# Relative attention rows stored and loaded with 800 bytes, the constant end filled on chip

## What is computed

```python
q, k, v = proj(Wq, bq), proj(Wk, bk), proj(Wv, bv)          # [B, 16, L, 16]
attn = einsum('bhld,bhrd->bhlr', q, k) * scale
dist = clip(arange(L)[None, :] - arange(L)[:, None], -64, 8) + 64
rel  = einsum('bhld,lrd->bhlr', q, dist_emb[dist]) * scale   # 73 different values a query
attn = softmax(attn + rel, axis=-1)
x = layernorm(x + (attn @ v) @ Wo.T + bo)
```

## Time and profile before

| | |
|---|---|
| median of 3 runs | 1431.49 us (1430.58 to 1434.02) |
| the profiled execution | 1432.69 us, its span 1430.9 us |
| TensorE (PE) busy | 1272.6 us, 89% |
| VectorE (DVE) busy | 1043.6 us, 73% |
| ScalarE (ACT) busy | 947.5 us, 66% |
| GpSimd (POOL) busy | 337.1 us, 24% |
| mean granted TensorE clock | 0.951 |
| moved by DMA | 273.13 MB, mean 191 GB/s |

### The profile page before, as it was taken

How to read it: one execution, slowest core, us unless ns; L and a number is a source line. 1 busy time by engine, 2 the same in 40 slices (tenths; PEclk the granted TensorE clock), 3 DMA queues, 4 the chain that set the end, 5 groups by cost and what they waited for, 6 DMA issues and landing times. The chain is left out here.

```text
span 1430.9 us, 24911 instructions
## 1 busy us (share of the span) xinstructions
PE 1272.6 (89%) x8220; PEld 675.3 (47%) x8220; DVE 1043.6 (73%) x2547; ACT 947.5 (66%) x1666; POOL 337.1 (24%) x567
## 2 busy tenths in 40 slices
PE   7788999999999999999999999999996899910597
PEld 4334344344334334334434434437885687700586
DVE  3366788888887888888888888862574467999655
ACT  4434677777777777777777777773765558959600
POOL 4544121211211211212112121004553002310012
PEclk9988999999999999999999999999998799965799
DMA  8999977878888788698797786625321314825032
GB/s 240 300 339 253 255 222 220 229 206 245 224 221 226 215 244 214 201 265 215 209 251 208 233 223 183 206 75 168 98 71 45 133 59 130 311 87 207 11 108 88
DMA packets 263758, 273.13 MB, mean 191 GB/s; under 512 B 66222, under 2 KB 246990, under 8 KB 259534
## 3 DMA queue, kind: packets, MB, share of 16 engines
q1 hardware_dynamic: 261998, 268.39, 64.7%
q10 hardware_dynamic: 1632, 3.15, 0.7%
HBM read 153.69 MB, written 117.00 MB: 189 GB/s over the span
## 5 line engine op out<-in xcount | busy, mean ns | idle before, releaser
L604 ACT ACTIVATE pr<-scoresT 128x512 f32<-128x512 f32 x1024 | 548.4, 600 | 210.5 <-PE scoresT L856 151.3
L851 PE MATMUL scoresT<-qT,kT 99*128 99x512 bf16 (+7 forms) x1408 | 357.2, 327 | 5.5 <-DVE attn_out L741 2.3
L701 DVE TENSOR_REDUCE mx<-scores_for_max 128x1 f32<-128x888 f32 (+6 forms) x448 | 301.7, 673 | 0.0
L696 DVE CUSTOM_DVE_ANT_0 junk<-scores_for_max,win 128x200 f32<-128x200 f32 (+2 forms) x512 | 180.0, 352 | 158.3 <-PE scores_for_max L823 149.1
L699 DVE TENSOR_REDUCE mx<-scores_for_max 128x1 f32<-128x64 f32 (+6 forms) x448 | 277.5, 619 | 0.0
L869 PE MATMUL attn_out<-pr,vS 128*17 128x512 f32 x2048 | 270.3, 600 | 4.4 <-DMA vS<-v_all 4.2
L851 PEld LDWEIGHTS scoresT<-qT,kT 99*128 99x128 bf16 (+1 forms) x1408 | 107.9, 98 | 334.0 <-ACT rows L581 97.0
L856 PE MATMUL scoresT<-idf,win 128*128 128x128 f32 (+1 forms) x1024 | 201.7, 258 | 0.0
L478 POOL COPY rows<-rows 128x736 f32<-128x736 f32 x128 | 102.5, 800 | 379.3 <-ACT rows L581 379.3
L822 PE MATMUL scores_for_max<-kX,qT 64*128 64x512 bf16 x512 | 167.2, 384 | 3.9 <-DVE mx L701 3.0
L823 PE MATMUL scores_for_max<-kX,qX 64*128 64x512 bf16 x512 | 167.2, 384 | 0.0
(11 more groups left out here) (203 smaller groups left out, 1728.2 us busy)
## 6 DMA issues: line engine op xcount, KB each, us to landing
rel_table<-rows SPq DMA_DIRECT2D x128, 512.0 KB, 4.7
win<-rel_table SPq DMA_DIRECT2D x128, 512.0 KB, 5.4
up_raw<-xT_normed SPq DMA_DIRECT2D x6, 1536.0 KB, 9.2
xT_normed<-up_raw SPq DMA_DIRECT2D x6, 1536.0 KB, 6.6
qT<-q_parts SPq DMA_DIRECT2D x32, 256.0 KB, 7.6
kX<-k_parts SPq DMA_DIRECT2D x64, 128.0 KB, 5.0
kT<-k_parts SPq DMA_DIRECT2D x32, 256.0 KB, 5.6
q_parts<-shared SPq DMA_DIRECT2D x32, 192.0 KB, 4.7
```

Source lines behind the costliest of these rows:

```text
L604: nc.scalar.activation(pr[:, n % NPR, h, :], bank, ACT.Exp).then_inc(t_read, 1)
L696: last = nc.vector.tensor_tensor_reduce(junk[:, n % 2, 0:z - a], bank[:, a:z], win[:, T % NW, q4, h, u:u + z - a], 1.0, NEG, ALU.add, ALU. ...
L701: last = nc.vector.tensor_reduce(mx[:, T % 2, q4, h, 2:3], bank[:, z:L], AX.X, ALU.max)
L851: last = mm(bank[:, a:e], k[0:r], q[0:r, a:e], start=(n == 0), stop=not near and n == len(pieces) - 1, skip_group_check=True)
```

## The change

LP goes from 184 to 128, so a row tile has 200 places a head (NC) in place of 256 and a row of the table 328 in place of 384. A store of a row tile and a load of a window move 800 bytes a row in place of 1024. The loaded 200 values stand at places 56 to 255 of `win` (FLAT = 56). Places 0 to 55 are filled by GpSimd with the value at place 56, for the 72 queries (partitions) that the `before` matmul reads, within shift_of. Those who read the constant at place 0 read it at place 56. `cut_window` and the first score of a tile wait for the fill (w_flat). For the fourth `side` tile, `cut` now also lies 72 queries in, as for the other three: the product is split into 456 and 56 queries, and the transposing matmul has 72 queries.

```diff
--- before.py
+++ after.py
@@ -53,10 +53,11 @@
     LEAD = 8
     CH = 16
     WRAP = RIGHT
-    LP = 184
+    LP = 128
     NC = LP + NJ
     TWID = NC + P
     WID = 2 * P
+    FLAT = P - LEFT - WRAP
     VW = HD + 1
     NEG = -3.0e38
     BLKS = 2 * B
@@ -130,6 +131,7 @@
         o_rec = sem("o_rec")
         r_padded = sem("r_padded")
         w_cut = sem("w_cut")
+        w_flat = sem("w_flat")
         m_left = sem("m_left")
         m_top = sem("m_top")
         m_small = sem("m_small")
@@ -311,8 +313,8 @@
                     sp.wait_ge(st_row[j], 16 * (T + 1))
                 for h in range(G):
                     first = ((T % 2 * G + h) * HALF) * TWID + P
-                    src = bass.AP(tab.tensor, first, [[TWID - 1, P], [P * TWID, 4], [1, WID]])
-                    sp.dma_start(win[:, T % NW, :, h, :], src).then_inc(ld_w[T % NW], 16)
+                    src = bass.AP(tab.tensor, first, [[TWID - 1, P], [P * TWID, 4], [1, WID - FLAT]])
+                    sp.dma_start(win[:, T % NW, :, h, FLAT:WID], src).then_inc(ld_w[T % NW], 16)
 
             def store_row(T, j):
 
@@ -480,17 +482,20 @@
             def cut_window(T):
 
                 pool.wait_ge(m_top, T + 1)
+                pool.wait_ge(w_flat, T + 1)
                 cut = win[:, T % NW, 0, :, 0:P - WRAP] if T % 2 == 0 else win[:, T % NW, 3, :, WID - WRAP:WID]
                 nc.gpsimd.memset(cut, 0.0).then_inc(w_cut, 1)
 
             def shift_of(T):
 
-                w = win[:, T % NW, :, :, 0]
+                w = win[:, T % NW, :, :, FLAT]
                 parts = [mcol[:, T % 2, :, 0:6 * G].rearrange("p q (h v t) -> p v q h t", v=2, t=3)[:, :, :, :, t] for t in range(3)]
                 both = shift[:].rearrange("p v (q h) -> p v q h", h=G)
                 rest = srem[:].rearrange("p v (q h) -> p v q h", h=G)
                 pool.wait_ge(ld_w[T % NW], 16 * G * (T // NW + 1))
                 link(nc.gpsimd.tensor_scalar(both[:, 1], w, -1.0, None, ALU.mult))
+                ends = win[0:SIDE, T % NW].rearrange("p q h n -> p (q h) n")
+                nc.gpsimd.tensor_copy(ends[:, :, 0:FLAT], ends[:, :, FLAT:FLAT + 1].to_broadcast([SIDE, 16, FLAT])).then_inc(w_flat, 1)
                 pool.wait_ge(m_top, T + 1)
                 if T >= 2:
                     pool.wait_ge(t_full, entries_to("shift", T - 2, 0))
@@ -702,7 +707,7 @@
                 last.then_inc(x_read, 1)
                 if c == CH - 1:
                     dve.wait_ge(x_read, n + 1)
-                    nc.vector.tensor_tensor(mx[:, T % 2, :, :, 3], mx[:, T % 2, :, :, 0], win[:, T % NW, :, :, 0], ALU.add).then_inc(m_left, 1)
+                    nc.vector.tensor_tensor(mx[:, T % 2, :, :, 3], mx[:, T % 2, :, :, 0], win[:, T % NW, :, :, FLAT], ALU.add).then_inc(m_left, 1)
                     if T:
                         dve.wait_ge(m_ready, T)
                     dve.wait_ge(m_left, T + 1)
@@ -829,6 +834,7 @@
                     pe.wait_ge(sh_in[hf], 16 * G * (i + 1))
                     pe.wait_ge(ld_k[i % 2], 16 * 4 * (i // 2 + 1))
                     pe.wait_ge(ld_w[T % NW], 16 * G * (T // NW + 1))
+                    pe.wait_ge(w_flat, T + 1)
                 if kt == TL - 1 and h == 0:
                     pe.wait_ge(w_cut, T + 1)
                 bank = bank_for("score", T, G * kt + h)
@@ -839,7 +845,7 @@
                 side = (kt + 1) % TL - 4 * hf
                 if kt == TL - 1 and hf == 1:
                     cut = 0
-                elif 0 <= side < 3:
+                elif 0 <= side < 4:
                     cut = side * P + SIDE
                 else:
                     cut = min(max((side + 1) * P, 0), HALF)
```

## The result

The changed kernel took 1444.57 us (median of 4 runs, 1443.77 to 1446.27), the kernel before, run beside it, 1432.35 (median of 4, 1430.58 to 1434.02). The ratio estimated from all the runs of both is 1.0078 (95%: 1.0066 to 1.0091); the two medians alone, 12.2 us apart, give 1.0085. The changed kernel is slower. The forecast was slower too, but by 4.4 us, with 1443 as the upper end of its range, which 1444.57 exceeds. The profiled execution took 1443.94 us and its span is 1442.2, against 1432.69 and 1430.9.

The account below looks back on a forecast made before the run. TensorE was taken to bound the attention loop, with transfers holding it up in the projections before. Fill +11.3, side tile -0.9 and transfers -6.0 gave +4.4 us, so 1435.9 us from a median of 1431.49; range 1426 to 1443.

Parts of the forecast that it names:

- The last turn (tile 30): Last turning of the shifts in the attention: the fill delays it by 0.88 us, with no shorter pad_row giving time back.
- The transfers (-6.0): Row stores and window loads at 800 bytes: shorter TensorE waits ahead of the loop, -6.0 us (0 to -10).
- the 2.0 and the 2.8: Projections: TensorE's wait for the queries loses 2.0 us of 10.15, its wait for the values 2.8 of 4.24.
- the line through the earlier trace: DMA cost of a packet: 39 ns at 800 bytes against 48 at 1024, a saving of 8.6 ns.
- the rival (no gain at all): Transfers buy nothing: 800-byte packets cost what 1024 did, or issue and latency pace the landing; 1442 us, chance 0.15.
- The 1.2 that the prediction put on the clock: Behind the value wait: a shorter stall may keep TensorE's clock up, half of that gain counted, 1.2 us.
- The turns in the loop: Turning of the shifts: the 0.93 us fill makes 14 even tiles 0.70 us later each, 9.8 us.
- odd tiles just covered: Odd tiles in the loop: 0.70 us spare at the turn nearly absorbs the fill, 0.2 us for 15 tiles.
- The rival of a cheap fill: Fill on GpSimd needs no more than about 0.35 us, so the kernel is faster, 1426 us; chance 0.15.
- The side tile (-0.9): Fourth side tile's split matmuls: heads 0.43 us apart in place of 0.44, -0.9 us (-5.1 to +2.0).
- 9.8 + 0.4 + 0.2: Fill's delay outside the last turn: even tiles 9.8 us, tile 0's turn in the projections 0.4, odd tiles 0.2.

Follow-up runs that it names:

- e3: Changed kernel with the fill moved behind the step that sets m_ready in the last turn only: 1439.85 us, 1.0044 of the kernel before.
- e6: Changed kernel with VectorE's first dequantising made to wait for the last turn's shifts, fill left in place: 1441.03 us, 1.0054 of the kernel before.
- e5: Kernel before with 800-byte rows and short pads, side tiles unchanged, fill over 128 partitions behind the last small step: 1429.93 us, 0.9980 of the kernel before.
- e7: Changed kernel run once more with no edit: 1444.14 us, 1.0076 of the kernel before.
- e4: Kernel before with only the fourth side tile cut to 72 queries: 1433.62 us, 0.9997 of the kernel before.
- e1: Changed kernel with the fill moved behind the last small step in every tile: 1428.98 us, 0.9969 of the kernel before.
- e8: Changed kernel with the small steps ahead of pad_row of row tiles three and four, fill and cut_window after both: 1430.17 us, 0.9977 of the kernel before.
- e2: Kernel before with only the fill and its waits added, 1024-byte transfers, pads and side tiles as before: 1453.76 us, 1.0145 of the kernel before.

## Why the forecast had the sign and not the size

**The step that failed** is "The last turn (tile 30) has no pad_row ahead of it: 0.88". Its premise was that each small step keeps its 0.3 us wherever the fill pushes it. They were pushed under VectorE's dequantising and took 1.82 and 0.92. From the 31st turn to the end of the attention the trace of after has 59.49 - 55.39 = 4.1 us more. From the 31st to the 32nd turn, the last, it takes 28.66 in place of 25.70, which is 3.0 us; the other 1.1 come behind the last turn, where the clock has fallen. Shown from two sides: with the fill moved in this one tile (e3) the 4.2 us go, and with VectorE's work moved (e6) the steps are short again.

**The transfers (-6.0)** were the second miss, nearly as large: -2.9 measured (e5), and some of that is the shorter pad_row. What failed in the sum is the 2.0 and the 2.8 that the two waits were to lose. The packets did get cheaper, though by less than forecast. The queue's share fell from 64.7% of 1430.9 us to 60.6% of 1442.2, 51.8 us; times 16 engines over the 131,072 packets that changed that is 6.3 ns a packet, where the line through the earlier trace rows gave 8.6. And a saved microsecond of DMA time is not a saved microsecond of waiting: both waits fell by 0.9 in after, and the value wait goes from 1.4 to 6.9 us between executions. Of the rival (no gain at all), the part that an 800-byte packet costs what 1024 did is ruled out by the queue's share. That none of it reaches the time is unlikely by e5 but not excluded, since e5 holds the shorter pad_row as well; what paces the landing of these loads stays open. The 1.2 that the prediction put on the clock can't be told apart either: the clock behind the value wait held at 1.00 where that wait was 1.39 (e7) and 1.96 us (e6), and fell in after, with 3.32.

**The turns in the loop** came out as forecast: the fill 0.93 us, m_ready 0.66 later (0.70), odd tiles just covered. 8.35 us over 26 tiles, with the side tile's -0.6 out of it, is 9.0 for the 13 even turns, 0.69 each. The rival of a cheap fill is out: the copy of 896 elements takes 927 ns over 72 partitions and 929 over 128 (e5).

**The side tile (-0.9)**: 0.43 us a head as forecast, -0.4 us in the times within their ±1.3.

The sum by these estimated ratios, as one microsecond is 0.0007 of the time: last turn +4.6 (e7 less e3), transfers -2.9 (e5), side tile -0.4 (e4), and what is left of +10.9 (e7) is +9.6 for the other turns, where the prediction had 9.8 + 0.4 + 0.2 = 10.4. So of the miss of 6.5 us +3.7 is the last turn, +3.1 the transfers, +0.5 the side tile, and -0.8 the other turns. Each ratio carries 1.3 to 2 us of uncertainty, and the differences more, so only the first two stand clear of zero, and the -0.8 does not; for the last turn the traces give 4.1, +3.2 above the forecast. Against the forecast time there is also +0.9 that is in no term: the kernel before had a median of 1432.35 beside the changed one, not 1431.49. The 1.3 us left of the 8.7 between 1435.9 and 1444.57 are the distance from e7's +10.9 to the +12.2 of the first two medians, which is inside their noise.

**Not a cost of the change:** the 2.1 us behind the attention in the trace of after. From the end of the attention to the end of the span the traces have between 465.2 and 467.6 us; e4, whose loop runs as before, has 467.60, and e7 466.84. What makes this part vary wasn't looked for.

## What to carry to other kernels

When an edit delays an engine by a fixed time, look at every place where the delayed instructions run, the last iteration above all, and at what the neighbouring engine does in the microsecond that follows: here the last step in the kernel before began 0.26 us ahead of a blocking instruction, and missing it once cost as much as six ordinary turns. Work that only the next stage needs belongs behind the signal that the busiest engine waits for; the same fill four instructions later turned +0.8% into -0.3%. Put the gain of a lighter transfer at what the busy engine's wait for it loses over several executions, not at what the packets save.

## What the runs showed of the hardware

- GpSimd and VectorE held each other up here to the end of the instruction that was under way: a 0.29 us CAST took 1.82 beside a 1.76 us TENSOR_TENSOR with two SBUF inputs, a 0.30 us step took 0.92 beside a 0.96 us TENSOR_SCALAR, and a VectorE TENSOR_SCALAR took 0.32 in place of 0.19 beside GpSimd's fill. Where the fill started first, the TENSOR_TENSOR took 2.46 or 2.47 in place of 1.76 (e1, e3, e5, e8). e6 shows the first two by taking VectorE's work away. Not every instruction does it: the fill took its 0.93 us beside VectorE's 1.70 us TENSOR_REDUCE in after.
- The granted clock fell after a short idle time of TensorE at the last turn. From 940 to 950 us it is 0.83 in after and in e7, where TensorE had stood 3.39 us in after; in e6 it is 0.83 from 941 to 951 behind an idle time of only 1.24 us. In e3 the turn waits 0.37 us. The lines of e6 and of e3:

```profile
941.00:951.00 10.00, 9.55 (x57) 2.46 (x58) 9.60 (x10) 6.78 (x13) 0.04 (x2) 0.83 0.01 3
...
940.00:950.00 10.00, 8.74 (x60) 2.54 (x60) 9.73 (x10) 8.26 (x17) 2.69 (x8) 1.00 0.08 16
```

So the clock stays full in e3, as it does from 400 to 600 us in after, where turns wait 0.6 us. A wait like that of after is paid twice: 3.0 us as waiting and 1.1 at the lower clock. The shorter wait of e6 has the same 1.1 us behind it. The length of the wait alone does not decide, though: all ten traces have the wait of 2.3 us ahead of the loop, and behind it (128 to 136 us) the clock is 1.00 in after, e1, e3, e6 and e8 and between 0.62 and 0.79 in the kernel before, e2, e4, e5 and e7. All five that hold it have 800-byte rows, but so do e5 and e7, so whether the change has a part in that is not shown.
- A GpSimd copy over 72 partitions costs what its elements per partition say (896: 927 ns; 512: 611 ns and 736: 800 ns with 128 partitions), with the sixteen short runs of a broadcast value costing nothing extra.
